# Second edge stage of a graph network: source rows gathered with an add onto spread destination rows in SBUF

## The chip, the cores and the metric

One core of one Trainium2 chip runs the whole program. The time is that of the device, in microseconds, for one execution from inputs in HBM to the output in HBM; the kernel before takes 10617.58 us (median of 3 runs, 10607.35 to 10631.53). Engines are named as in the profile: PE is TensorE, DVE VectorE, ACT ScalarE, POOL GpSimd, SP SyncE, which only issues transfers here.

## The reference, cut to what matters

Two message-passing layers on 12,500 nodes of 160 numbers (64 scalars, 32 vectors of 3) and 200,000 edges sorted by destination. The change lies in the second layer's edge stage, an equivariant attention:

```python
ms = src_s[edge_src] + dst_s[edge_dst]          # per edge: source row + destination row
mv = src_v[edge_src] + dst_v[edge_dst]
w = h @ rw3 + roff                              # weights of the edge, h from an MLP of 64 edge scalars
o0a = w1 * ms
o0b = w4 * (jnp.einsum('eud,ed->eu', mv, Y1) / SQ3)
o1a = (w2 * ms)[:, :, None] * Y1[:, None, :]
o1b = w3[:, :, None] * mv
o1c = w5[:, :, None] * (jnp.cross(mv, Y1[:, None, :]) / SQ2)
ls, lv = _eq_lin(ds, dv, lin_ws, lin_bs, lin_wv)  # ds, dv: the o's side by side
a = jnp.einsum('ehk,hk->eh', _smooth_leaky(alpha), alpha_dot)   # then softmax over the edges of a node
ns = jax.ops.segment_sum(vs * a[..., None], edge_dst, num_segments=n)
```

The two sums of the first lines, 160 numbers per edge, are what is made in another way.

## The kernel before, in words

The stages follow one another: first edge stage (up to about 3530 us), node update (to about 5650 us), second edge stage (5653 to about 9900 us), last node update. The second edge stage is `layer1_edges`. Its edges, padded, are 1568 tiles of 128 edges (R = 128, one edge per SBUF partition). Four tiles (GT = 4) are a sub-batch, eight sub-batches (STEPS = 8) a pass, 49 passes the stage: 392 sub-batches. The first and the last pass are written out, the other 47 are one loop whose body holds eight sub-batches; `At(t, r)` is sub-batch r of pass t, `i.plus(2)` the one two later, and `i.n(...)` the count that a semaphore has to reach.

Nothing schedules this code. Each engine has its own `body`, in program order, and semaphores alone set how the engines stand to one another. `gate` waits for something that has long been true. For one sub-batch i the engines do this:

- SP loads, four sub-batches ahead, the windows `e_win` of destination rows (table TD; L1831, L1832), for every other one h (`e_h`, L1844), and indices and the like now and then; it stores the totals of older sub-batches.
- DVE makes selection matrices (`e_pick`, L1951) for sub-batch i+3.
- PE spreads the destination rows of i+2 over their edges: a selection times a window (`spread_out`, L2124) in two halves of two tiles each, 128 x 320 into PSUM.
- ACT copies each half to SBUF (`keep_far`, L2252), into `e_rows[:, p, 1]`, p being the sub-batch's parity.
- POOL issues four indirect gathers (L1933), one per tile, of 128 source rows of 160 floats (table TS) into `e_rows[:, p, 0]`, and then one multiplication (`weighted`, L1917) for sub-batch i-8. Before the gathers it waits for `added` of i-2, the sign that DVE has used this half of `e_rows`.
- DVE's `sums` adds the two halves of `e_rows` to `e_m` (L1961, 128 x 640, sets `added`), then makes products and cross products with the edge's direction (L1966 to L1974). It does so for i+1. Its `results` for i-1 takes PE's output apart (L2014 to L2030), `weigh` (L1986 to L1992) multiplies PE's weights with `e_m` into `e_d` (sets `d_ready`), and `members` makes `e_q` (L2004).
- PE, after the spreads, turns back the outputs of i-1 (`turn_back`, L2173), makes the weights of i+1 from `e_h` (L2110), waits for `d_ready` of i, turns `e_d` in three groups of transposes (`turn`, L2135), with the totals of i-6 (L2149) between, and applies the linear maps (L2156, L2162, L2163).
- ACT copies out of PSUM: `e_dT` three times and `e_oT` twice (`keep`, L2261), the results (L2281, L2285) and the totals (L2272).

PE's two first groups of `turn` wait for `far_kept` of i+2, since the spreads and the transposes share PSUM banks. What PE, ACT and DVE do follows PE's order closely; POOL's gathers of i are used by DVE two sub-batches later at most.

Of the kernel before, what the change touches and what calls it, by code (L numbers as in the profile page):

```python
# [112 lines left out]
def gate(eng, k):  # L113


    eng.wait_ge(k["ready"], 4)
# [1624 lines left out]
def layer1_edges(nc, m, k, ps, W, TS, TD, index, LR, BASE, iota, dstI, rows_dst, heads_dst, H, yx, TOT):  # L1741

    own = ExitStack()
    with own:
# [7 lines left out]
        hh = sb("e1_h", [128, 2, GT * R])  # L1752
        rows = sb("e1_rows", [R, 2, 2, GT, X])
        m_ = sb("e1_m", [R, 2, GT, X])
        prod, cA, cB, cr = (sb("e1_" + n, [R, GT, 3, V]) for n in ("prod", "cA", "cB", "cr"))
# [11 lines left out]
            "at_here", "row_here", "dh_here", "h_here"))  # L1767
        rows_here = [sem(f"e1_rows_here{p}") for p in range(2)]
        local_here, base_here = ([sem(f"e1_{n}{p}") for p in range(2)] for n in ("local_here", "base_here"))
# [3 lines left out]
        stored = [sem(f"e1_stored{s}") for s in range(STEPS)]  # L1773
        ones_set, added, crossed, mixed, w_ready, d_ready, turned, kept, mapped, outs, by_y, freed = (sem("e1_" + n) for n in (
            "ones_set", "added", "crossed", "mixed", "w_ready", "d_ready", "turned", "kept", "mapped", "outs", "by_y", "freed"))
        silued, logit, xT, apart, masked, forward, scanned, mT, shifted = (sem("e1_" + n) for n in (
# [24 lines left out]
        with nc.Block() as block:  # L1801
            @block.sync
            def _(sp):
# [53 lines left out]
                def body(t):  # L1857
                    final = isinstance(t, int) and t == PASSES - 1
                    for r in range(STEPS):
                        i, ahead = At(t, r), At(t, r).plus(4)  # L1860
                        if ahead.within():
                            gate(sp, k)
                            sp.wait_ge(spread, ahead.n(2, 2, 4))
                            load_windows(ahead)
                        if r % 4 == 0 and not final:
                            load_base(r // 4, t + 1)
                        if r % 4 == 1 and not final:
                            gate(sp, k)
                            sp.wait_ge(picked, i.n(1, 3))
                            load_local(r // 4, t + 1)  # L1870
                        if not (final and r >= 6):
                            gate(sp, k)
                            sp.wait_ge(w_ready, i.n(1, 1))
                            load_h(r % 2, t * 4 + (r // 2 + 1))
                        if r % 4 == 3 and not final:
                            gate(sp, k)
                            sp.wait_ge(added, i.n(1, 1))
                            load_at(r // 4, t + 1)
                        if r % 4 == 2 and not i.before(4) and not (final and r == 6):
                            gate(sp, k)  # L1880
                            sp.wait_ge(scanned, i.groups(0))
                            load_dh(1 - r // 4, t + r // 4)
                        if r % 4 == 1 and not i.before(9):
                            gate(sp, k)
                            sp.wait_ge(q_ready, i.n(1, 1, 6))
                            load_row(r // 4, t)
                        if not i.before(6):
                            gate(sp, k)
                            store(i, 6)
# [19 lines left out]
            def _(pool):  # L1909
# [10 lines left out]
                def body(t):  # L1920
                    for r in range(STEPS):
                        i, p, gp = At(t, r), r % 2, r // 4
                        if r % 4 == 0:
                            gate(pool, k)
                            pool.wait_ge(at_here[gp], i.uses(16, 16))
                        if not i.before(2):
                            gate(pool, k)
                            pool.wait_ge(added, i.n(1, 1, 2))
                        pool.sem_inc(begun, 1)
                        gate(pool, k)  # L1930
                        for c in range(GT):
                            col = 4 * (r % 4) + c
                            pool.indirect_dma_start(rows[:, p, 0, c, :], None, TS, bass.IndirectOffsetOnAxis(  # L1933
                                ap=at[:, gp, col:col + 1], axis=0)).then_inc(rows_here[p], 16)
                        if not i.before(8):
                            weighted(i, 8)
# [5 lines left out]
            def _(dve):  # L1942
# [11 lines left out]
                def sums(i):  # L1954

                    p = i.r % 2
                    gate(dve, k)
                    dve.wait_ge(rows_here[p], i.uses(256, 64 * (i.r // 2) + 64))
                    gate(dve, k)
                    dve.wait_ge(far_kept, i.n(2, 2))  # L1960
                    dve.tensor_tensor(m_[:, p], rows[:, p, 0], rows[:, p, 1], ALU.add).then_inc(added, 1)  # L1961
                    gate(dve, k)
                    dve.wait_ge(added, i.n(1, 1))
                    vec = m_[:, p, :, S:X].rearrange("n c (i u) -> n c i u", i=3)
                    y = [bc(yx[:, j:j + 3, bass.ds(i.n(4), GT)].rearrange("n i c -> n c i"), V, 3) for j in range(3)]
# [10 lines left out]
                def weigh(i):  # L1976

                    p = i.r % 2
                    gate(dve, k)
                    dve.wait_ge(w_ready, i.n(1, 1))  # L1980
                    if not i.before(2):
                        gate(dve, k)
                        dve.wait_ge(turned, i.n(5, 3, 2))
                    vec = m_[:, p, :, S:X].rearrange("n c (i u) -> n c i u", i=3)
                    to = d[:, p].rearrange("r c j x -> r c (j x)")[:, :, S + 128:384].rearrange("r c (i a u) -> r c i a u", i=3, a=2)
                    dve.tensor_tensor(d[:, p, :, 0:2, 0:S], w4[:, :, 0:128].rearrange("r c (a u) -> r c a u", a=2),  # L1986
                                      bc(m_[:, p, :, 0:S], 2, 2), ALU.mult)
                    dve.tensor_tensor(to[:, :, :, 0], bc(w4[:, :, 128:160], 3, 2), vec, ALU.mult)
# [72 lines left out]
                def body(t):  # L2061
                    for r in range(STEPS):
# [4 lines left out]
                        if r % 4 == 1 and not i.before(5):  # L2067
                            scans(i)
                        if i.plus(3).within():
                            selections(i.plus(3))  # L2070
                        if not i.before(1):
# [14 lines left out]
                dve.wait_ge(ones_set, 2)  # L2086
                for r in range(3):
                    selections(At(0, r))
# [10 lines left out]
            def _(pe):  # L2099
# [27 lines left out]
                def turn(i, j):  # L2127
                    p = i.r % 2
                    gate(pe, k)
                    if j < 2 and i.plus(2).within():  # L2130
                        pe.wait_ge(far_kept, i.plus(2).n(2, j + 1))
                    else:
                        pe.wait_ge(kept, i.n(5, j - 1))
# [55 lines left out]
                def body(t):  # L2189
                    for r in range(STEPS):  # L2190
                        i, after = At(t, r), At(t, r + 1) if r + 1 < STEPS else At(t + 1, 0)
                        if i.plus(2).within():
                            spread_out(i.plus(2), 0, far2(i, 0), (far_kept, 3) if i.before(1) else (kept, i.n(5, -1)))
                        if not i.before(1):
                            turn_back(i.plus(-1), 0)
                        if i.plus(2).within():
                            spread_out(i.plus(2), 1, far2(i, 1), (far_kept, 4) if i.before(1) else (kept, i.n(5)))
                        if not i.before(1):
# [19 lines left out]
                pe.wait_ge(ones_set, 2)  # L2218
                for r in range(2):
                    for half in range(2):  # L2220
                        spread_out(At(0, r), half, far2(At(0, 0), half), (far_kept, half + 1) if r else None)
                weights(At(0, 0))
# [10 lines left out]
            def _(act):  # L2233
# [12 lines left out]
                def keep_far(i, half, of):  # L2246
                    gate(act, k)
                    act.wait_ge(spread, i.n(2, half + 1))
                    if half == 0 and not i.before(2):
                        gate(act, k)  # L2250
                        act.wait_ge(added, i.n(1, 1, 2))
                    act.activation(rows[:, i.r % 2, 1, 2 * half:2 * half + 2, :], of, ACT.Copy).then_inc(far_kept, 1)  # L2252

# [33 lines left out]
                def body(t):  # L2287
                    for r in range(STEPS):
                        i = At(t, r)
                        if i.plus(2).within():  # L2290
                            keep_far(i.plus(2), 0, far2(i, 0))
                            keep_far(i.plus(2), 1, far2(i, 1))
                        if not i.before(1):
# [13 lines left out]
                act.preload_act_table_set("exp_and_others")  # L2307
                for r in range(2):
                    for half in range(2):
                        keep_far(At(0, r), half, far2(At(0, 0), half))  # L2310
# [828 lines left out]
```

## Time and profile before

| | |
|---|---|
| median of 3 runs | 10617.58 us |
| profiled execution, first to last instruction | 10684.3 us |
| PE busy | 8950.9 us, 84% |
| DVE busy | 8008.3 us, 75% |
| POOL busy | 6686.3 us, 63% |
| ACT busy | 4828.6 us, 45% |
| mean granted clock of TensorE | 0.925 |

The profiled execution has no time of its own beside the span; the span is 66.7 us above the median of the timed runs. The busy columns are sums over stages with different limits, so they don't say what bounds the second edge stage; the windows view cuts it out. In the rows, "idle before, releaser" is idle time of an engine just before an instruction and what ended it; such a releaser is inferred from semaphore events, and a transfer that has long been over can be named by mistake. The columns of the timeline are start, duration, engine, line, operation, and in brackets the idle time ahead.

### The profile page before, as it was taken

The page shows a single profiled execution, that of the slowest core. Times are in us where ns is not written, and L with a number is a line of the kernel's source. Part 1 is how long each engine was busy: PE and PEld are TensorE (multiplying, and loading weights), DVE is VectorE, ACT ScalarE, POOL GpSimd, SP SyncE. Part 2 cuts the span into 40 slices and gives each one's busy share as a digit, 9 for nine tenths or more (in the row PEclk, how much of TensorE's full clock was granted, in tenths as well). Part 3 has the DMA queues.
Part 4 walks back from the last instruction along what each step waited for, and adds up shares of the span by engine and source line. Part 5 has one row for each costly group of instructions (what it writes and reads, how often), then busy time and mean ns, then how long its engine had stood idle before and what let it go on. Part 6 is the DMA issues. An engine that isn't in the chain of part 4 may idle for free. (4 is left out here: it accounts for less than half of the span.)

```text
span 10684.3 us, 192482 instructions
## 1 busy us (share of the span) xinstructions
PE 8950.9 (84%) x34728; PEld 5257.6 (49%) x34728; DVE 8008.3 (75%) x15400; ACT 4828.6 (45%) x9073; POOL 6686.3 (63%) x4771
## 2 busy tenths in 40 slices
PE   0888888888888799999986888888888888888588
PEld 0444444444444222223225666666666666666233
DVE  3277777777777688888877888888888888888455
ACT  0276666666666211111113444444444444444255
POOL 4488888888888788888873444444444444444231
PEclk5599999999999899999988999999999999999699
DMA  5588888888888999999973444444444444444222
GB/s 202 172 168 171 168 163 169 165 166 169 167 163 162 208 228 224 223 233 230 227 165 105 121 121 121 120 124 124 121 121 122 121 126 121 120 121 123 56 68 52
DMA packets 1081323, 1616.13 MB, mean 151 GB/s; under 512 B 218498, under 2 KB 831885, under 8 KB 1025357
## 3 DMA queue, kind: packets, MB, share of 16 engines
q1 hardware_dynamic: 755862, 1273.87, 43.7%
q0 software_dynamic: 325056, 338.58, 20.2%
q14 instruction: 361, 2.96, 0.1%
q8 instruction: 44, 0.72, 0.0%
HBM read 1533.80 MB, written 444.07 MB: 185 GB/s over the span
## 5 line engine op out<-in xcount | busy, mean ns | idle before, releaser
L442 POOL DMA_INDIRECT sums<-e_total,e_place x1568 | 2493.7, 1590 | 584.8 <-DMA sums<-e_total,e_place 313.9
L1933 POOL DMA_INDIRECT e_rows<-TS,e_at x1568 | 1542.7, 984 | 1738.0 <-DVE e_m L1961 1174.4
L579 PE MATMUL ps<-e_win,e_pick 128*128 128x448 f32 x3136 | 1341.6, 573 | 159.6 <-DVE e_u L476 105.9
L579 PEld LDWEIGHTS ps<-e_win,e_pick 128*128 128x128 f32 x3136 | 620.4, 203 | 917.7 <-issue 832.9
L2261 ACT ACTIVATE e_dT<-ps 128x512 f32<-128x512 f32 x1176 | 671.1, 597 | 841.2 <-PE ps L2135 353.3
L2135 PE MATMUL ps<-ident,e_d 128*128 128x128 f32 x4704 | 663.1, 278 | 300.6 <-ACT e_dT L2261 289.6
L1917 POOL TENSOR_TENSOR e_val<-e_val 128x640 f32<-128x640 f32 x392 | 511.5, 1306 | 523.7 <-ACT e_val L2238 518.0
L1094 POOL TENSOR_TENSOR n_zv<-n_zv,n_ast 128x1536 f32<-128x1536 f32 x200 | 762.9, 3814 | 120.0 <-DMA n_zv<-in_x_groups 107.7
L1299 PE MATMUL ps<-n_z,w_uss 128*64 128x512 f32 x1600 | 748.6, 612 | 20.8 <-DVE n_z L1142 20.1
L2261 ACT ACTIVATE e_oT<-ps 128x512 f32<-128x512 f32 x784 | 469.1, 598 | 627.1 <-PE ps L2163 454.9
L2149 PE MATMUL ps<-e_val,e_q 128*128 128x168 f32 x3136 | 630.7, 327 | 127.6 <-ACT e_tot L2272 108.0
L2135 PEld LDWEIGHTS ps<-ident,e_d 128*128 128x128 f32 x4704 | 547.7, 142 | 382.1 <-ACT e_dT L2261 338.7
L742 DVE SCALAR_TENSOR_TENSOR r_y<-ps,w_rb,r_rstd 128x512 f32<-128x512 f32 x394 | 295.5, 750 | 576.7 <-issue 528.6
L2110 PE MATMUL ps<-w_r,e_h 128*128 128x224 f32 x3136 | 670.3, 357 | 53.5 <-issue 52.0
L2149 PEld LDWEIGHTS ps<-e_val,e_q 128*128 128x128 f32 x3136 | 517.0, 202 | 370.7 <-ACT e_tot L2272 225.5
L1098 POOL TENSOR_TENSOR n_zv<-n_zv 128x512 f32<-128x512 f32 x400 | 668.2, 1670 | 36.9 <-POOL n_zv L1094 0.4
L711 PE MATMUL ps<-r_sq,w_avg 128*128 128x512 f32 x788 | 453.4, 659 | 277.9 <-issue 277.9
L592 PEld LDWEIGHTS ps<-e_u,e_q 128*128 128x128 f32 x3136 | 540.7, 191 | 188.0 <-issue 188.0
L2124 PE MATMUL ps<-e_win,e_pick 128*128 128x160 f32 x3136 | 565.6, 304 | 72.7 <-issue 62.6
L2124 PEld LDWEIGHTS ps<-e_win,e_pick 128*128 128x128 f32 x3136 | 482.4, 194 | 246.8 <-issue 245.5
L620 ACT ACTIVATE e_far<-ps,attr 128x160 f32<-128x160 f32 x1176 | 442.8, 390 | 353.2 <-PE ps L579 214.8
L2110 PEld LDWEIGHTS ps<-w_r,e_h 128*128 128x128 f32 x3136 | 566.5, 191 | 72.3 <-issue 70.8
(438 smaller groups left out, 19874.2 us busy)
## 6 DMA issues: line engine op xcount, KB each, us to landing
e_win<-T SPq DMA_DIRECT2D x1568, 168.0 KB
n_z<-in_x_groups SPq DMA_DIRECT2D x400, 512.0 KB
n_zv<-in_x_groups SPq DMA_DIRECT2D x800, 192.0 KB
TOT<-e_tot SPq DMA_DIRECT2D x392, 352.0 KB
e_row<-in_src_rows SPq DMA_DIRECT2D x98, 1024.0 KB
e_local<-LR SPq DMA_DIRECT2D x196, 512.0 KB
e_row<-in_dst_rows SPq DMA_DIRECT2D x98, 1024.0 KB
e_win<-TD SPq DMA_DIRECT2D x1568, 60.0 KB
```

The costliest lines, as they stand in the source:

```text
L442: pool.indirect_dma_start(sums[c], bass.IndirectOffsetOnAxis(ap=place[:, r % 4, c:c + 1], axis=0), total[:, r % 4, c, 0:MSG0], None, compu ...
L579: pe.matmul(g[:, c, :], pick[:, p, R * c:R * c + R], win[:, s, c, :], start=True, stop=True).then_inc(spread, 1)
L592: last = pe.matmul(out[:, c, :], q[:, p, c, :], u[:, p, c, :], start=True, stop=True)
L1094: pool.tensor_tensor(zv[:, b], zv[:, b], ast[:, g.p], ALU.mult).then_inc(zv_ready, 1)
L1098: pool.tensor_tensor(zv[:, b, 0], zv[:, b, 0], zv[:, b, i], ALU.add).then_inc(zv_ready, 1)
L1299: last = pe.matmul(ps[0:S, U0, :], W["uss"][:, 4 * s + j, :], z[:, s % 4, j, :], start=False, stop=False)
L1933: pool.indirect_dma_start(rows[:, p, 0, c, :], None, TS, bass.IndirectOffsetOnAxis(ap=at[:, gp, col:col + 1], axis=0)).then_inc(rows_here[ ...
L2110: last = pe.matmul(w4[:, c, 0:224], hh[:, p, R * c:R * c + R], W["r3"][:], start=True, stop=True)
L2124: last = pe.matmul(to[:, c % 2], pick[:, p, R * c:R * c + R], win[:, s, c, :], start=True, stop=True)
L2135: last = pe.transpose(ps[:, bank(i, 2 + j), R * c:R * c + R], d[:, p, c, j, :], I[0:R, 0:R])
L2149: last = pe.matmul(tot2[:, c % 2], q[:, j % 2, c, :], val[:, slot // 4, 4 * (slot % 4) + c, :], start=True, stop=True)
L2261: act.activation(to, ps[:, bank(i, 2 + j), :], ACT.Copy).then_inc(kept, 1)
```

## The change

The tile `e_rows` and the semaphore `added` go. `e_m` gets four slots in place of two. ACT copies the spread destination rows straight into the sub-batch's slot of `e_m`. POOL's gathers wait until these copies are made, the first two tiles for the first half, the other two for the second, and write with an add (`compute_op=ALU.add`) onto the slot, so that the DVE instruction L1961 goes. ACT's copy waits for `d_ready` of the sub-batch four back, the last use of the slot. Spreads and their copies move from i+2 to i+3, selections from i+3 to i+4, with one more of each ahead of the first pass. SP's wait for `added` becomes one for `mixed`, which DVE sets after the cross products. Results are otherwise made as before.

```diff
-        rows = sb("e1_rows", [R, 2, 2, GT, X])
-        m_ = sb("e1_m", [R, 2, GT, X])
+        m_ = sb("e1_m", [R, 4, GT, X])
...
-        rows_here = [sem(f"e1_rows_here{p}") for p in range(2)]
+        rows_here = [sem(f"e1_rows_here{s}") for s in range(4)]
...
                         if r % 4 == 3 and not final:
                             gate(sp, k)
-                            sp.wait_ge(added, i.n(1, 1))
+                            sp.wait_ge(mixed, i.n(1, 1))
                             load_at(r // 4, t + 1)
...
-                        if not i.before(2):
-                            gate(pool, k)
-                            pool.wait_ge(added, i.n(1, 1, 2))
-                        pool.sem_inc(begun, 1)
-                        gate(pool, k)
                         for c in range(GT):
+                            if c % 2 == 0:
+                                gate(pool, k)
+                                pool.wait_ge(far_kept, i.n(2, c // 2 + 1))
+                                pool.sem_inc(begun, 1)
+                                gate(pool, k)
                             col = 4 * (r % 4) + c
-                            pool.indirect_dma_start(rows[:, p, 0, c, :], None, TS, bass.IndirectOffsetOnAxis(
-                                ap=at[:, gp, col:col + 1], axis=0)).then_inc(rows_here[p], 16)
+                            pool.indirect_dma_start(m_[:, r % 4, c, :], None, TS, bass.IndirectOffsetOnAxis(
+                                ap=at[:, gp, col:col + 1], axis=0), compute_op=ALU.add).then_inc(rows_here[r % 4], 16)
...
-                    dve.wait_ge(rows_here[p], i.uses(256, 64 * (i.r // 2) + 64))
-                    gate(dve, k)
-                    dve.wait_ge(far_kept, i.n(2, 2))
-                    dve.tensor_tensor(m_[:, p], rows[:, p, 0], rows[:, p, 1], ALU.add).then_inc(added, 1)
-                    gate(dve, k)
-                    dve.wait_ge(added, i.n(1, 1))
+                    dve.wait_ge(rows_here[s], i.uses(128, 64 * (i.r // 4) + 64))
...
-                        if i.plus(3).within():
-                            selections(i.plus(3))
+                        if i.plus(4).within():
+                            selections(i.plus(4))
...
-                    if j < 2 and i.plus(2).within():
-                        pe.wait_ge(far_kept, i.plus(2).n(2, j + 1))
+                    if j < 2 and i.plus(3).within():
+                        pe.wait_ge(far_kept, i.plus(3).n(2, j + 1))
...
-                    if half == 0 and not i.before(2):
+                    if half == 0 and not i.before(4):
                         gate(act, k)
-                        act.wait_ge(added, i.n(1, 1, 2))
-                    act.activation(rows[:, i.r % 2, 1, 2 * half:2 * half + 2, :], of, ACT.Copy).then_inc(far_kept, 1)
+                        act.wait_ge(d_ready, i.n(1, 1, 4))
+                    act.activation(m_[:, i.r % 4, 2 * half:2 * half + 2, :], of, ACT.Copy).then_inc(far_kept, 1)
```

In PE's and ACT's bodies `i.plus(2)` becomes `i.plus(3)` for `spread_out` and `keep_far` in the same way.

On POOL, the start of the loop's body, before. ISA and REGISTER_ALU are waits and register work; `x4` are the four gathers of a sub-batch.

```order
L1925 ISA
L1928 ISA
L1933 DMA e_rows<-TS,e_at 128x160 x4
L1915 ISA
L1917 TENSOR_TENSOR e_val<-e_val 128x32x20
```

The same place after the change:

```order
L1924 ISA
L1928 REGISTER_ALU
L1932 DMA e_m<-TS,e_at 128x160 x2
L1928 REGISTER_ALU
L1932 DMA e_m<-TS,e_at 128x160 x2
L1914 ISA
L1916 TENSOR_TENSOR e_val<-e_val 128x32x20
```

The four gathers keep their place ahead of the multiplication; they are now in two pairs, each behind a wait of its own.

On DVE, one sub-batch from the last instruction of `weigh` to the first of `results`, before:

```order
L1992 TENSOR_TENSOR e_d<-ps,e_dot 128x4x32
L1961 TENSOR_TENSOR e_m<-e_rows 128x640
L1966 TENSOR_TENSOR e_prod<-e_m,yx 128x384
L1967 TENSOR_TENSOR e_cA<-e_m,yx 128x4x64
L1968 TENSOR_TENSOR e_cA<-e_m,yx 128x4x32
L1969 TENSOR_TENSOR e_cB<-e_m,yx 128x4x32
L1970 TENSOR_TENSOR e_cB<-e_m,yx 128x4x64
L1973 TENSOR_REDUCE e_dot<-e_prod 128x128
L1974 TENSOR_TENSOR e_cr<-e_cA,e_cB 128x384
L1951 TENSOR_SCALAR e_pick<-e_local,nodes_sb 128x512
```

And after:

```order
L1986 TENSOR_TENSOR e_d<-ps,e_dot 128x4x32
L1960 TENSOR_TENSOR e_prod<-e_m,yx 128x384
L1961 TENSOR_TENSOR e_cA<-e_m,yx 128x4x64
L1962 TENSOR_TENSOR e_cA<-e_m,yx 128x4x32
L1963 TENSOR_TENSOR e_cB<-e_m,yx 128x4x32
L1964 TENSOR_TENSOR e_cB<-e_m,yx 128x4x64
L1967 TENSOR_REDUCE e_dot<-e_prod 128x128
L1968 TENSOR_TENSOR e_cr<-e_cA,e_cB 128x384
L1950 TENSOR_SCALAR e_pick<-e_local,nodes_sb 128x512
```

The add is gone and nothing else on DVE changes its place; the selection is that of one sub-batch later.

## Rows read from the trace of the kernel before

**Rows 1.** Windows: length, busy us (instructions) of PE, PEld, DVE, ACT, POOL, clock, DMA share, GB/s.

```profile
5660.00:9890.00 4230.00, 3633.11 (x19695) 2839.48 (x19696) 3570.15 (x8683) 2050.17 (x4481) 2043.68 (x1951) 0.97 0.43 121
```

**Rows 2.** Waits, 5660 to 9890: us in total, times, longest us.

```profile
POOL e_rows L1933 <- DVE e_m L1961: 1174.4, 332, 6.9
...
ACT e_dT L2261 <- PE ps L2135: 352.7, 256, 3.6
...
ACT e_dT L2261 <- DMA r_xT<-in_edge_attr: 320.0, 106, 4.1
PE ps L2135 <- ACT e_dT L2261: 289.6, 203, 2.6
...
ACT e_tot L2272 <- remote: 174.8, 95, 3.4
...
ACT e_silu L2281 <- DMA H<-r_h: 126.6, 68, 3.3
...
PE ps L2124 <- DMA e_win<-TD: 10.1, 2, 5.3
```

**Rows 3.** Timeline of one sub-batch of the second edge stage.

```profile
7575.33 1.10 POOL L1933 DMA_INDIRECT e_rows<-TS,e_at  x1 [4.69 <-DVE e_m L1961]
...
7576.83 1.68 PE L2110 MATMUL ps<-w_r,e_h 128*128 128x224 f32 x8
...
7578.35 1.04 PE L2135 MATMUL ps<-ident,e_d 128*128 128x128 f32 x8
...
7579.22 0.74 PE L2149 MATMUL ps<-e_val,e_q 128*128 128x168 f32 x4
7579.25 0.95 POOL L1933 DMA_INDIRECT e_rows<-TS,e_at  x1 [0.30 <-issue]
...
7579.87 0.42 DVE L2030 TENSOR_REDUCE e_val<-e_silu 128x32 f32<-128x256 f32 x1
...
7581.25 1.08 ACT L2261 ACTIVATE e_dT<-ps 128x512 f32<-128x512 f32 x2 [3.46 <-DMA r_xT<-in_edge_attr]
...
7581.35 0.69 DVE L1986 TENSOR_TENSOR e_d<-ps,e_m 128x512 f32<-128x512 f32 x1 [1.06 <-DMA r_xT<-in_edge_attr]
...
7581.90 0.66 PE L2135 MATMUL ps<-ident,e_d 128*128 128x128 f32 x4 [1.95 <-ACT e_dT L2261]
```

**Rows 4.** Timeline of the first edge stage, beside its indirect scatters.

```profile
2006.45 2.05 PE L711 MATMUL ps<-r_sq,w_avg 128*128 128x512 f32 x2 [2.89 <-issue]
...
2007.49 1.55 POOL L442 DMA_INDIRECT sums<-e_total,e_place  x1 [0.30 <-ACT e_total L633]
...
2008.58 0.69 ACT L727 ACTIVATE r_std<-ps,w_eps 128x512 f32<-128x512 f32 x1 [1.36 <-PE ps L711]
```

**Rows 5.** Groups by line, 5660 to 9890: busy, mean ns, idle before and releasers.

```profile
L1933 POOL DMA_INDIRECT e_rows<-TS,e_at x1563 | 1537.9, 984 | 1682.2 <-DVE e_m L1961 1174.4 <-issue 507.8
L1917 POOL TENSOR_TENSOR e_val<-e_val 128x640 f32<-128x640 f32 x388 | 506.2, 1305 | 502.7 <-ACT e_val L2238 497.0 <-issue 0.6
...
L1961 DVE TENSOR_TENSOR e_m<-e_rows 128x640 f32<-128x640 f32 x392 | 373.3, 952 | 0.0
```

**Rows 6.** Indirect scatters by line: duration ns min/median/max, first and last start.

```profile
L442 POOL DMA_INDIRECT sums<-e_total,e_place x1568: 1547/1552/2079, 503.1 to 3520.5; - x196
...
L1115 POOL DMA_INDIRECT TD<-n_rows,n_rank_of x100: 960/1001/2357, 3695.9 to 5597.8; - x100
```

**Rows 7.** DMA queues, 5660 to 9890, then 503 to 3530: packets, MB, share.

```profile
q0 software_dynamic: 75072, 128.22, 12.2%
...
q0 software_dynamic: 225792, 154.24, 47.9%
```

**Rows 8.** DVE L2027 alone, then an instance of it beside POOL's L1917.

```profile
L2027 DVE TENSOR_TENSOR e_silu<-e_silu,w_ad x392: 408/454/2125, 5691.3 to 9904.8; 128x256 f32<-128x256 f32 x196
...
7526.15 1.26 POOL L1917 TENSOR_TENSOR e_val<-e_val 128x640 f32<-128x640 f32 x1
7526.38 1.33 DVE L2027 TENSOR_TENSOR e_silu<-e_silu,w_ad 128x256 f32<-128x256 f32 x1
```

More of the change, by code:

```diff
@@ L1773, in layer1_edges @@
         stored = [sem(f"e1_stored{s}") for s in range(STEPS)]
-        ones_set, added, crossed, mixed, w_ready, d_ready, turned, kept, mapped, outs, by_y, freed = (sem("e1_" + n) for n in (
-            "ones_set", "added", "crossed", "mixed", "w_ready", "d_ready", "turned", "kept", "mapped", "outs", "by_y", "freed"))
+        ones_set, crossed, mixed, w_ready, d_ready, turned, kept, mapped, outs, by_y, freed = (sem("e1_" + n) for n in (
+            "ones_set", "crossed", "mixed", "w_ready", "d_ready", "turned", "kept", "mapped", "outs", "by_y", "freed"))
         silued, logit, xT, apart, masked, forward, scanned, mT, shifted = (sem("e1_" + n) for n in (
@@ L1921, in body @@
                     for r in range(STEPS):
-                        i, p, gp = At(t, r), r % 2, r // 4
+                        i, gp = At(t, r), r // 4
                         if r % 4 == 0:
@@ L1954, in sums @@
                 def sums(i):
-                    p = i.r % 2
+                    s = i.r % 4
                     gate(dve, k)
-                    dve.wait_ge(rows_here[p], i.uses(256, 64 * (i.r // 2) + 64))
-                    gate(dve, k)
-                    dve.wait_ge(far_kept, i.n(2, 2))
-                    dve.tensor_tensor(m_[:, p], rows[:, p, 0], rows[:, p, 1], ALU.add).then_inc(added, 1)
-                    gate(dve, k)
-                    dve.wait_ge(added, i.n(1, 1))
-                    vec = m_[:, p, :, S:X].rearrange("n c (i u) -> n c i u", i=3)
+                    dve.wait_ge(rows_here[s], i.uses(128, 64 * (i.r // 4) + 64))
+                    vec = m_[:, s, :, S:X].rearrange("n c (i u) -> n c i u", i=3)
                     y = [bc(yx[:, j:j + 3, bass.ds(i.n(4), GT)].rearrange("n i c -> n c i"), V, 3) for j in range(3)]
@@ L1976, in weigh @@
                 def weigh(i):
-                    p = i.r % 2
+                    p, s = i.r % 2, i.r % 4
                     gate(dve, k)
@@ L1983, in weigh @@
                         dve.wait_ge(turned, i.n(5, 3, 2))
-                    vec = m_[:, p, :, S:X].rearrange("n c (i u) -> n c i u", i=3)
+                    vec = m_[:, s, :, S:X].rearrange("n c (i u) -> n c i u", i=3)
                     to = d[:, p].rearrange("r c j x -> r c (j x)")[:, :, S + 128:384].rearrange("r c (i a u) -> r c i a u", i=3, a=2)
                     dve.tensor_tensor(d[:, p, :, 0:2, 0:S], w4[:, :, 0:128].rearrange("r c (a u) -> r c a u", a=2),
-                                      bc(m_[:, p, :, 0:S], 2, 2), ALU.mult)
+                                      bc(m_[:, s, :, 0:S], 2, 2), ALU.mult)
                     dve.tensor_tensor(to[:, :, :, 0], bc(w4[:, :, 128:160], 3, 2), vec, ALU.mult)
@@ L2086, in _ @@
                 dve.wait_ge(ones_set, 2)
-                for r in range(3):
+                for r in range(4):
                     selections(At(0, r))
@@ L2191, in body @@
                         i, after = At(t, r), At(t, r + 1) if r + 1 < STEPS else At(t + 1, 0)
-                        if i.plus(2).within():
-                            spread_out(i.plus(2), 0, far2(i, 0), (far_kept, 3) if i.before(1) else (kept, i.n(5, -1)))
+                        if i.plus(3).within():
+                            spread_out(i.plus(3), 0, far2(i, 0), (far_kept, 5) if i.before(1) else (kept, i.n(5, -1)))
                         if not i.before(1):
                             turn_back(i.plus(-1), 0)
-                        if i.plus(2).within():
-                            spread_out(i.plus(2), 1, far2(i, 1), (far_kept, 4) if i.before(1) else (kept, i.n(5)))
+                        if i.plus(3).within():
+                            spread_out(i.plus(3), 1, far2(i, 1), (far_kept, 6) if i.before(1) else (kept, i.n(5)))
                         if not i.before(1):
@@ L2218, in _ @@
                 pe.wait_ge(ones_set, 2)
-                for r in range(2):
+                for r in range(3):
                     for half in range(2):
-                        spread_out(At(0, r), half, far2(At(0, 0), half), (far_kept, half + 1) if r else None)
+                        spread_out(At(0, r), half, far2(At(0, 0), half), (far_kept, 2 * r + half - 1) if r else None)
                 weights(At(0, 0))
@@ L2289, in body @@
                         i = At(t, r)
-                        if i.plus(2).within():
-                            keep_far(i.plus(2), 0, far2(i, 0))
-                            keep_far(i.plus(2), 1, far2(i, 1))
+                        if i.plus(3).within():
+                            keep_far(i.plus(3), 0, far2(i, 0))
+                            keep_far(i.plus(3), 1, far2(i, 1))
                         if not i.before(1):
@@ L2307, in _ @@
                 act.preload_act_table_set("exp_and_others")
-                for r in range(2):
+                for r in range(3):
                     for half in range(2):
```

## The prediction

> **What bounds the kernel now.** I read the windows view first, to see which engine fills the stage that is changed. The second edge stage runs from 5660 to 9890 us, 4230 us for 392 sub-batches of four tiles, so 10.79 us each [rows 1]. TensorE (PE) is busy 3633 us of it, 9.27 us per sub-batch, at a granted clock of 0.97, the upper level of 2.4 GHz but for 3%. VectorE (DVE) is busy 9.11 us, GpSimd (POOL) 5.21 us, ScalarE (ACT) 5.23 us. So PE is nearest to the bound and stands idle for 1.52 us per sub-batch; what the change is worth is decided by what happens to those 1.52 us, since PE's own 9.27 us stay.
>
> Next I read the waits of that stage, to see what PE's idle time ends with. PE waits for ACT's copies (L2261), 290 us in 203 of the sub-batches [rows 2]. It hardly waits for DVE: no such row is near the top. ACT in turn waits 353 us for PE's transposes (L2135), and 320, 175 and 127 us are put down to transfers of the first edge stage or to nothing named ("r_xT", "remote", "H"). Those transfers ended long before, so these are semaphore events whose sender the trace could not pair. They sum to 622 us, 1.59 us per sub-batch, which is PE's idle time over again.
>
> The timeline of one sub-batch says what they are [rows 3]. PE ends its two groups of transposes (L2135) at 7579.39. ACT should copy them at once, but starts at 7581.25 after 3.46 us of idling, and DVE, which needs PE's products of L2110 (ended 7578.51), starts e_d at 7581.35, though its last reduction was over by about 7580.3. PE, which needs ACT's copies, stands from 7579.96 to 7581.90. Both late starts come 1.05 to 1.15 us after POOL's last gather instruction ended (7579.25 + 0.95 = 7580.20). So: while the four gathers of a sub-batch flow, PE's finished work is told late to its consumers, and it is told about 1 us after the last gather was issued. I call this the hold. Beside the first edge stage's indirect scatters it is not seen: there a PE matmul (L711) ends at 2008.50 while a scatter is under way, and its consumer on ACT starts at 2008.58 [rows 4].
>
> **The change, part by part.**
>
> *The add on DVE goes.* 392 x 952 ns = 373 us of DVE's time [rows 5], 0.95 us per sub-batch. Nothing on PE waits for DVE as it is, so at 10.79 us per sub-batch it is worth 0; it would count only if PE's loss went first (rival 1). DVE's next limit is then 9.11 - 0.95 = 8.16 us busy.
>
> *The gathers become accumulating ones.* The trace has no gather with an add. A plain gather takes POOL 984 ns; the nearest row with an add is the first stage's scatter (L442), 1552 ns as median, 1590 as mean, while a plain scatter (L1115) takes 1001 ns [rows 5, 6]. I take 1.55, with bounds of 0.95 (the add is free on POOL) and 2.5 (the longest plain scatter, 2.36 [rows 6], rounded up). With 0.30 us from one to the next [rows 3, 4] four take 7.40 us instead of 4 x 1.25 = 5.0 us, and with the weighting L1917 (1.26 + 0.30) POOL comes to 8.96 us of 10.79: it still fits.
>
> *Their transfers.* 5660 to 9890: the software queue has 12.2% of 16 engines, 0.122 x 16 x 4230 / 1563 = 5.28 engine-us per gather of 80 KB. The accumulating scatters: 0.479 x 16 x 3027 / 1568 = 14.8 for 96 KB, 12.3 scaled to 80 KB [rows 7]. The DMA share goes from 0.43 to about 0.12 x 12.3/5.28 + 0.31 = 0.59: not a bound, and a gather's share of the 16 engines (0.77 us) is shorter than its issue.
>
> *The order of arrival.* POOL now waits for ACT's copies of the same sub-batch instead of DVE's add of the one two before. POOL waited 1174 us for that add [rows 2], so it was early anyway. Behind the waiting gather stand on POOL the other gathers and L1917, whose product PE wants two sub-batches on. The gathered rows are needed by DVE's sums two sub-batches on, over 10 us later: no loss. ACT's copy waits for d_ready four sub-batches back, long past; the rings hold.
>
> *One sub-batch further ahead.* PE's spread (L2124), ACT's copy and DVE's selection have the same count and place, only a later sub-batch as object; the first pass has one more of each ahead of it, about 3 us once, in which POOL no longer gathers. The windows are asked for by SP four sub-batches ahead and now needed one earlier. They are waited for 10 us in all now, the last of [rows 2]; I take 0 to 0.1 us per sub-batch.
>
> *The hold.* This is the term that decides. The train of four gathers lasts now from 7575.33 to 7580.20, 4.87 us. With 1.55 us each it lasts 4 x 1.55 + 3 x 0.30 = 7.10 us, 2.23 more; its first issue ends 0.60 later, so that the stretch in which PE's news is late grows by 1.6 us. As much as 1.6 us per sub-batch could be lost once more; now the loss is 1.52 us on a stretch of 4.87 + 1.05 - 1.10 = 4.8 us, a third, and a third of 1.6 is 0.5. PE waits for ACT in 203 of 392 sub-batches [rows 2], about half: half of 1.6 is 0.8, to which I add 0.1 for sub-batches newly caught and for the windows. Value taken: 0.9 us, x 392 = 353 us. Bounds: 0.3 (the longer stretch falls mostly on PE's long runs without a consumer) and 2.1 (all of 1.6, and 0.5 of stalls of DVE beside L1917, which now follows the last gather at another place: L2027 took 1.33 us beside it in place of 0.45 [rows 8]).
>
> Here the Trainium skill speaks against my reading. *SBUF — State Buffer*, section *Who interferes with whom*, has it that DMA never contends with a compute engine and that "PE and ACT never wait on anyone". In rows 3 ACT starts 1.86 us after PE's end and within 1.1 us of the last gather's, which no port explains; if the rule covered semaphores too, the lateness would be something else's, the longer train would cost nothing, and the result would be rival 2's. The trace here does not agree with so wide a reading of it.
>
> **Sum.** Beside the profiled execution, 10684.3 us of span and 66.7 us (0.6%) above the median of the runs, it is 10684 + 353 = 11037; against the median it is 10617.6 + 353 = **10,970 us**. With its bounds, 118 to 823 us: 10,740 to 11,440.
>
> **The rivals.**
>
> *Rival 1, faster: the accumulating gathers hold nothing.* The scatters with an add don't [rows 4], plain gathers do, and an accumulating gather is as much of the one as of the other. Then PE's loss of 1.52 us mostly goes. The floors are PE 9.27, POOL 8.96, DVE 8.16 plus its dependences; with 0.6 us left of ordinary waits the period is 9.9: -0.89 x 392 = -350 us, 10,270 us. For it: the hold was seen only beside gathers that write SBUF without an add. Against it: these write SBUF too, and the train is longer.
>
> *Rival 2, no change: the hold keeps its size or isn't the gathers'.* If it follows the bytes (80 KB each, unchanged) rather than the issue time, all terms are hidden: 10,600, within 60.
>
> *Rival 3, slower still: POOL becomes the bound.* 4 x (t + 0.30) + 1.56 passes 10.79 at t = 2.0 us. The plain scatter has a maximum of 2.36 [rows 6]. At t = 2.5 the period is 12.8, +2.0 x 392 = +780 us, 11,400 us. Every us over the threshold counts fourfold.
>
> **Chances.** Forecast 0.50, rival 1 0.27, rival 2 0.18, rival 3 0.05. A difference under 0.2%, 21 us, can't be told from none. The forecast and rival 3 are slower whole; rival 1 is faster whole; rival 2 I split 0.08 faster, 0.06 same, 0.04 slower. That makes faster 0.35, same 0.06, slower 0.59. The likeliest case's own range is 10,740 to 11,440; with rival 1's middle 10,260 to 11,450, which leaves out the faster half of rival 1 and the end of rival 3.
>
> **What would show it.** In the profile after: the gather with a mean near 1.55 us on POOL (under 1.1: the add is free, and the train is as before; over 2.0: rival 3, POOL near 100%); the software queue's share near 28% in this stage; DVE's busy time lower by 373 us; PE's the same 3633 us. The forecast is right if PE idles 2.4 us per sub-batch, the mislabelled waits of ACT grow to near 2.5 us per sub-batch, and ACT's late copies still start about 1 us after the last gather of each train. It is wrong if ACT starts within 0.2 us of PE's end while gathers are under way (rival 1), or if the period stays at 10.8 with the train at 7.1 us (rival 2).

## The result, and the profile after

The changed kernel takes 10058.99 us (median of 4 runs, 10040.0 to 10064.59), against 10616.4 for the kernel before: 0.947 of it, 95% interval 0.9457 to 0.9484. Forecast were 10,970 us and 3.3% more; it is 5.3% less. Rival 1 came closest, and even its 10,270 us lies 210 us too high. Timed once more among the experiments, the changed kernel came to 0.948 of before (0.9458 to 0.9505).

The windows view of the kernel after, columns as in [rows 1]:

```profile
5660.00:9300.00 3640.00, 3433.72 (x19723) 2780.57 (x19723) 3518.78 (x8308) 2092.36 (x4487) 3080.42 (x1956) 1.00 0.64 142
```

The stage is over some 600 us earlier. PE is busy almost throughout, at the upper clock level all the time (1.00, was 0.97), DVE too, and POOL, half idle before, is now full but for the gaps between its instructions. The gathers' tile says how the period fell: from (9867.9 - 5653.3) / 391 = 10.78 us to (9274.5 - 5662.3) / 391 = 9.24 us. Columns as in [rows 6], before and after:

```profile
L1933 POOL DMA_INDIRECT e_rows<-TS,e_at x1568: 942/949/1262, 5653.3 to 9867.9; - x196
...
L1932 POOL DMA_INDIRECT e_m<-TS,e_at x1568: 1540/1566/1982, 5662.3 to 9274.5; - x196
```

The waits of the kernel after, 5660 to 9270, columns as in [rows 2]:

```profile
POOL e_m L1932 <- issue: 461.5, 1531, 2.1
ACT e_dT L2255 <- PE ps L2129: 353.2, 289, 2.4
...
PE ps L2129 <- ACT e_dT L2255: 2.0, 5, 0.4
```

The waits of [rows 2] that named transfers of another stage, "r_xT", "remote" and "H", 622 us in all, are not in the list any more, and PE's 290 us of waiting for ACT have become 2. That is the lateness of PE's news, gone. The timeline of one sub-batch shows PE and ACT beside the accumulating gathers:

```profile
7583.02 1.82 POOL L1932 DMA_INDIRECT e_m<-TS,e_at  x1 [0.62 <-issue]
...
7584.44 1.04 PE L2129 MATMUL ps<-ident,e_d 128*128 128x128 f32 x8
...
7585.08 1.09 ACT L2255 ACTIVATE e_dT<-ps 128x512 f32<-128x512 f32 x2 [1.23 <-PE ps L2129]
7585.15 1.89 POOL L1932 DMA_INDIRECT e_m<-TS,e_at  x1 [0.31 <-issue]
```

ACT begins to copy the first group while PE still turns the second, in the middle of the train of gathers; in [rows 3] it began 1.86 us after PE had ended both. Over the whole trace it is the same: of the 1176 copies of e_dT none starts more than 0.1 us after both PE's group and ACT's own instruction before it have ended. In the kernel before 261 start more than 0.5 us late, the latest 3.1 us.

Last, the groups by line, 6000 to 9000, where DVE's e_q is new among the long ones:

```profile
L1998 DVE TENSOR_TENSOR e_q<-e_row,dstI 128x512 f32<-128x512 int32 x324 | 575.6, 1776 | 0.0
...
L1916 POOL TENSOR_TENSOR e_val<-e_val 128x640 f32<-128x640 f32 x324 | 552.9, 1707 | 60.5 <-ACT e_val L2232 60.5
```

e_q took 0.73 us before (`L2004`), the multiplication 1.30 [rows 5]. They now stand beside each other in about three of four sub-batches (e_q is over 0.9 us in 258 of 335 between 5900 and 9000 us), and it is e_q that waits. One such place:

```profile
7589.44 1.56 POOL L1932 DMA_INDIRECT e_m<-TS,e_at  x1 [0.30 <-issue]
...
7589.87 2.97 DVE L1998 TENSOR_TENSOR e_q<-e_row,dstI 128x512 f32<-128x512 int32 x1
...
7590.43 1.85 POOL L1916 TENSOR_TENSOR e_val<-e_val 128x640 f32<-128x640 f32 x1
```

The multiplication's record begins 0.57 us before that of the last gather ends (7591.00). From there it takes 1.28 us, and in every sub-batch from 5900 to 9000 between 1.25 and 1.29: its mean of 1.71 is the overlap of two records of POOL, not a slower multiplication.

### The profile page after: what moved, and what is told of

It reads as the page before. It is cut to its first block and busy times, and to the rows that moved or that the text cites. A ratio compares the mean times of both kernels' runs of the same rounds, so it can differ in the third digit from the quotient of the medians.

```text
span 10062.5 us, 191932 instructions
## 1 busy us (share of the span) xinstructions
PE 8731.8 (87%) x34728; PEld 5186.5 (52%) x34728; DVE 7958.4 (79%) x15008; ACT 4874.1 (48%) x9073; POOL 7733.9 (77%) x4771
## 5 line engine op out<-in xcount | busy, mean ns | idle before, releaser
L1932 POOL DMA_INDIRECT e_m<-TS,e_at x1568 | 2582.3, 1647 | 529.2 <-issue 462.4
L1916 POOL TENSOR_TENSOR e_val<-e_val 128x640 f32<-128x640 f32 x392 | 667.0, 1702 | 101.1 <-ACT e_val L2232 101.1
L1098 POOL TENSOR_TENSOR n_zv<-n_zv 128x512 f32<-128x512 f32 x400 | 689.4, 1723 | 36.8 <-POOL n_zv L1094 0.4
L1998 DVE TENSOR_TENSOR e_q<-e_row,dstI 128x512 f32<-128x512 int32 x392 | 684.6, 1747 | 13.3 <-PE ps L2143 13.3
L2129 PE MATMUL ps<-ident,e_d 128*128 128x128 f32 x4704 | 641.9, 273 | 3.5 <-ACT e_dT L2255 2.0
L2143 PEld LDWEIGHTS ps<-e_val,e_q 128*128 128x128 f32 x3136 | 496.8, 193 | 198.0 <-issue 153.4
L2143 PE MATMUL ps<-e_val,e_q 128*128 128x168 f32 x3136 | 586.1, 310 | 8.0 <-ACT e_tot L2266 7.5
L592 PE MATMUL ps<-e_u,e_q 128*128 128x194 f32 x3136 | 583.7, 329 | 0.0
```

What stands on the lines that cost most here:

```text
L592: last = pe.matmul(out[:, c, :], q[:, p, c, :], u[:, p, c, :], start=True, stop=True)
L1098: pool.tensor_tensor(zv[:, b, 0], zv[:, b, 0], zv[:, b, i], ALU.add).then_inc(zv_ready, 1)
L1916: pool.tensor_tensor(u[:, :, 1:SEG], u[:, :, 1:SEG], bc(u[:, :, 0], SEG - 1, 2), ALU.mult).then_inc(u_ready, 1)
L1932: pool.indirect_dma_start(m_[:, r % 4, c, :], None, TS, bass.IndirectOffsetOnAxis(ap=at[:, gp, col:col + 1], axis=0), compute_op=ALU.add). ...
L1998: dve.tensor_tensor(q[:, j % 2], row[:, gp, R * cols.start:R * cols.stop].rearrange("r (c e) -> r c e", c=GT), bc(dstI[:, 0, bass.ds(i.n(4 ...
L2143: last = pe.matmul(tot2[:, c % 2], q[:, j % 2, c, :], val[:, slot // 4, 4 * (slot % 4) + c, :], start=True, stop=True)
```

## The experiments

All ratios are to the kernel before on the same chip, with 95% intervals; a point is 1% of the time before. The period is read from the count of a line in a window of 3000 us. The diffs show the lines that change, shortened. "Late copies" are counted over each whole trace as above: copies of e_dT, of 1176, that start more than 0.5 us after both PE's group and ACT's instruction before have ended.

**Is it the kind of gather?** `e1_after_plain` leaves the add out of the gathers.

```diff
-   ap=at[:, gp, col:col + 1], axis=0), compute_op=ALU.add).then_inc(rows_here[r % 4], 16)
+   ap=at[:, gp, col:col + 1], axis=0)).then_inc(rows_here[r % 4], 16)
```

> The changed kernel with gathers that don't add: they overwrite the spread rows, so the destination rows are missing from the sums. All else (ring of four, spreads three ahead, POOL's waits on ACT's copies, no add on DVE) stays. Theory K (the kind of transfer: a plain gather holds PE's news, an accumulating one doesn't): the hold is back, PE idles again by about 1.5 us per sub-batch; period about 10.3 to 10.8, total 10,480 to 10,650 us. Rival O (the new order, waits and ring removed the loss): the stage stays at 9.2 us per sub-batch or falls, since a gather takes POOL 0.98 us in place of 1.65: 9,900 to 10,060 us.

Measured: 1.031 (1.0293 to 1.0328). Neither range of the expectation holds it: theory K had 10,480 to 10,650 us, and it is 11,010, slower than the kernel before. The new order with plain gathers loses 3.1%, and the late news is back, with 402 late copies. Timeline of it:

```profile
7581.73 1.04 PE L2129 MATMUL ps<-ident,e_d 128*128 128x128 f32 x8
7582.36 0.60 ACT L2255 ACTIVATE e_dT<-ps 128x512 f32<-128x512 f32 x1 [1.28 <-issue]
...
7584.13 0.95 POOL L1932 DMA_INDIRECT e_m<-TS,e_at  x1 [0.30 <-issue]
7584.65 0.60 ACT L2255 ACTIVATE e_dT<-ps 128x512 f32<-128x512 f32 x1 [1.70 <-PE ps L2129]
```

PE's second group ended at 7582.77, and ACT copies it at 7584.65, with the last gather of the train issued at 7584.13. POOL now starts behind ACT's copy of the spreads, so that the train should stand at the same critical place each time: ACT waits for PE's transposes 425 times up to 9200 us, 256 in [rows 2]. That this place is the reason for the extra loss was not tried.

`e2_before_add` puts the add into the gathers of the kernel before; their tile is cleared once, ahead of the stage, and nothing else changes.

```diff
-   ap=at[:, gp, col:col + 1], axis=0)).then_inc(rows_here[p], 16)
+   ap=at[:, gp, col:col + 1], axis=0), compute_op=ALU.add).then_inc(rows_here[p], 16)
...
+   for p in range(2):
+       pool.memset(rows[:, p, 0], 0.0).then_inc(cleaned, 1)
+   pool.wait_ge(cleaned, 2)
```

> The kernel before with an add in its gathers (onto e_rows' own half, cleared once, so the rows pile up and the values are not the reference's); DVE's add, its waits and the ring of two stay. Theory K: the hold goes, PE no longer idles for it; what is left is DVE with its add, 8.98 + 0.95 = 9.9 us per sub-batch, total 10,150 to 10,350 us. Rival O: the loss stays and the longer trains add to it, 10,620 us or more.

Measured: 1.005 (1.0031 to 1.0065): no gain from the gathers alone. The number is rival O's, its reason isn't: the loss did not stay, there are no late copies. Neither theory named what took its place; groups by line, 6000 to 9000:

```profile
L2008 DVE TENSOR_TENSOR e_q<-e_row,dstI 128x512 f32<-128x512 int32 x274 | 657.1, 2398 | 0.0
```

e_q has 2.40 us in place of 0.73. DVE is busy 2886 of 3000 us; it sets the period of 10.95 us, with PE at 9.4.

**Is it the spacing?** `e3_before_paced`: plain gathers, a fill on POOL after each.

```diff
+   if not (i.before(1) and c == 0):
+       gate(pool, k)
+       pool.wait_ge(filled, i.n(4, c))
+       pool.sem_inc(begun, 1)
+       gate(pool, k)
...
+   pool.memset(filler[:], 0.0).then_inc(filled, 1)
```

> The kernel before with plain gathers, but after each of them POOL fills a 128x256 tile nobody reads, so that a gather starts only every 1.9 to 2.2 us, as the accumulating ones do. Theory K: plain gathers hold at any pace; over a longer stretch, no gain: 10,620 to 11,100 us (this is also the step of my forecast, a longer train costs more: 10,900). Rival P (pace: the hold comes from gathers that follow each other too closely): most of the gain appears, 10,100 to 10,350 us.

Measured: 0.984 (0.9817 to 0.9857), 1.6% faster, against theory K and against the step of my forecast, and less than rival P. There are no late copies, but DVE is busy 2879 of 3000 us: POOL's multiplication now falls beside DVE's add (1.26 us in place of 0.95) and e_prod (1.23 in place of 0.56). The clean comparison needs DVE relieved; it is `e9_after_plain_paced`, the kernel of e1 with the same edit and a fill of 64 columns.

> The changed kernel with plain gathers (the destination rows are overwritten and missing, as in e1_after_plain, which took 1.031 of before) and after each a fill of 128x64 on POOL, so that they start about every 2.0 us in place of 1.3. Theory P (the spacing of the gathers, not their kind, decides whether PE's news is late): the hold goes, 0.945 to 0.965 of before, close to the changed kernel's 0.947. Rival K (the kind): 1.00 to 1.05.

Measured: 0.944 (0.9408 to 0.9467). POOL and ACT in its timeline:

```profile
7579.35 0.96 POOL L1939 DMA_INDIRECT e_m<-TS,e_at  x1 [3.35 <-issue]
7580.31 0.17 POOL L1941 MEMSET e_filler<- 128x64 f32 x1
...
7581.31 0.95 POOL L1939 DMA_INDIRECT e_m<-TS,e_at  x1 [0.82 <-POOL e_filler L1941]
...
7584.22 1.04 PE L2137 MATMUL ps<-ident,e_d 128*128 128x128 f32 x8
...
7584.86 1.09 ACT L2263 ACTIVATE e_dT<-ps 128x512 f32<-128x512 f32 x2 [1.19 <-PE ps L2137]
```

Same gathers, same order of everything else as e1; only 2.0 to 2.1 us from start to start in place of 1.3: 1.031 becomes 0.944, a little better even than theory P's range, and 402 late copies become none (the latest is 0.2 us late). Theory P holds, theory K falls: no accumulating gather is needed for the gain; it is slower to issue, and so spaced. How close is too close, `e14_plain_pairs` asks, with the fill after the second and fourth gather only (`if c % 2 == 1:`).

> As e9_after_plain_paced (plain gathers, destination rows missing, a start every 2.0 us, 0.944 of before), but POOL's fill of 128x64 only after the second and the fourth gather: they follow in pairs, 1.3 us within a pair and 2.0 us between. Theory P with all gathers counting alike: half the cost of close gathers comes back, 0.98 to 1.00. Rival: two close gathers hold nothing, only a train of four does: 0.935 to 0.95, POOL having more time. Other rival: one close pair is as bad as four: 1.02 or more.

Measured: 0.957 (0.9551 to 0.9583), between e9 and e1 and in none of the three ranges expected: of the 8.7 points from e9 to e1 pairs bring back 1.3. There are 11 late copies. A train of four close ones costs far more than two trains of two.

The late copies also settle a rival of the spacing, that the fills only move the train to a place where it does no harm. In e14 259 of PE's groups came due after the third gather, the first of the second pair, and none was copied late; in the kernel before 167 came due after the third gather of the train, and 129 were.

**What is DVE's add worth?** `e5_before_noadd` cuts it to two columns in the kernel before, `e6_paced_noadd` in e3; the sums are then constants, set once.

```diff
-   dve.tensor_tensor(m_[:, p], rows[:, p, 0], rows[:, p, 1], ALU.add).then_inc(added, 1)
+   dve.tensor_tensor(m_[:, p, :, 0:2], rows[:, p, 0, :, 0:2], rows[:, p, 1, :, 0:2], ALU.add).then_inc(added, 1)
...
+   dve.memset(m_[:], 1.0)
```

> The kernel before with DVE's add cut to two columns of each tile (the products then read constants: the sums are left out). Gathers stay plain and quick, one every 1.3 us. What the first runs left as theory PD: two limits lie over each other, the hold of PE's news (gone as soon as gathers start about 2 us apart) and DVE (with its add 10 us per sub-batch once it also stalls beside POOL). Then taking the add alone gives nothing: 0.98 to 1.01 of before. Rival A: the add was the main cost, most of the gain of 5.3% appears: 0.95 to 0.97.

> The same cut of the add, with the plain gathers spaced by POOL's fills as in the third run (which alone gave 0.984). No accumulating transfer, no ring of four, no spread further ahead is in it. Theory PD: both limits are gone, period 9.2 to 9.5 us, 0.945 to 0.96 of before, as the whole change. Rival K2: something of the change itself (the kind of transfer, the ring, the lead) is needed: 0.97 to 0.99.

Measured: 0.989 (0.9867 to 0.991) and 0.962 (0.9602 to 0.9642). The add alone is worth 1.1%, more than the nothing that I had, less than rival A; the late news stays in e5 (279 late copies). With spacing it is worth 2.2 points (0.984 to 0.962), with no late copies. e6 misses 0.945 to 0.96 by a little: with fills of 256 columns its gathers start 2.1 to 2.25 us apart, and the next train 3.3 us after the fourth, which makes up the period of 9.8 us; and POOL's multiplication falls beside DVE's e_cA, 1.56 us in place of 0.42. `e7_after_extra_add` gives the changed kernel such an add back, unread.

```diff
+   dve.tensor_tensor(extra[:], m_[:, s], m_[:, s], ALU.add).then_inc(added, 1)
+   gate(dve, k)
+   dve.wait_ge(added, i.n(1, 1))
```

> The changed kernel with an extra DVE addition of 128x640 ahead of the products, where before had its add, with the same wait behind it; nobody reads its result. Theory PD: DVE goes from 9.07 to over 10 us per sub-batch and sets the period: 10.1 to 10.9 us, 0.98 to 1.01 of before. Rival B: POOL, full at 4 x 1.95 + 1.4 us, is the bound of the changed kernel and DVE's stalls beside it are slack: below 0.965.

Measured: 0.962 (0.9592 to 0.9644), just inside rival B's range and far from theory PD's. 0.54 us of the add's 0.86 show in the period; e_q's mean falls from 1.78 to 1.33 us at the same time, so that a part of the add fills what was a stall.

**The stall beside POOL's multiplication.** `e11_before_add_w_small` and `e10_after_w_small` cut the multiplication in e2 and in the changed kernel.

```diff
-   pool.tensor_tensor(u[:, :, 1:SEG], u[:, :, 1:SEG], bc(u[:, :, 0], SEG - 1, 2), ALU.mult
+   pool.tensor_tensor(u[:, :, 1:3], u[:, :, 1:3], bc(u[:, :, 0], 2, 2), ALU.mult
```

> The kernel before with accumulating gathers (e2_before_add, 1.005 of before at 10.96 us per sub-batch, DVE busy 10.7 with 1.5 us of stall in e_q beside POOL's multiplication), with that multiplication cut in the same way. Theory S (the gain was hidden by that stall, since POOL's wait for DVE's add puts the multiplication beside e_q): DVE falls to 9.2 to 9.5, 0.955 to 0.975 of before. Rival (the ring of two or the order of waits costs it): above 0.985.

> The changed kernel with POOL's multiplication cut from 20 to 2 columns of each head (most of the weighting is left out). It gives back about 1 us per sub-batch on POOL and DVE's stall of 1.0 us in e_q beside it. Theory Q (POOL is the bound of the changed kernel, with PE's 8.75 us just under it): period 8.8 to 8.95, 0.93 to 0.94 of before. Rival (PE's chain is the bound): 0.944 to 0.95.

Measured: 0.948 (0.9446 to 0.9508) in place of 1.005, better than theory S's range, and 0.940 (0.9368 to 0.9425) in place of 0.947, the edge of theory Q's. Group by line of e11:

```profile
L2008 DVE TENSOR_TENSOR e_q<-e_row,dstI 128x512 f32<-128x512 int32 x324 | 242.5, 748 | 0.0
```

With e_q back at 0.75 us the kernel before, given accumulating gathers, runs as fast as the changed one with its add on DVE still there. So the stall hid the gain in e2. In the changed kernel it and POOL's fullness cost 0.7%. (The cut also frees 0.7 to 0.8 us of POOL; the two aren't told apart.)

**Versions meant to be faster.** Three put the multiplication elsewhere in POOL's order: `e4_after_mid` ahead of the third gather, `e13_after_w_c3` ahead of the fourth (both in three of four sub-batches), `e12_three_one` behind the second, which is plain and added by DVE. `e8_hybrid` takes two gathers plain, the second and the fourth, and DVE adds them. The edit of e4:

```diff
+   if c == 2 and r % 4 != 0 and not i.before(8):
+       weighted(i, 8)
...
-   if not i.before(8):
+   if r % 4 == 0 and not i.before(8):
        weighted(i, 8)
```

> The changed kernel with POOL's multiplication moved between the second and the third gather in three of four sub-batches, away from DVE's e_q (L1998), which takes 1.77 us in place of 0.74 since both read SBUF. Theory D (after the change POOL and DVE bound each other: POOL is full, DVE 97%): e_q falls to below 1.1 us, the multiplication to 1.3, period 9.21 to about 9.0, total 9,950 to 10,010 us. Rival: PE with 8.8 us busy and its chain sets the period, total within 20 us of 10,059.

> The changed kernel with POOL's multiplication ahead of the fourth gather in three of four sub-batches, so that it should fall beside DVE's weigh, whose instructions read one operand from PSUM, and not beside e_q. e10_after_w_small (0.940) is what could be had at most. Theory S (what the multiplication meets on DVE decides): e_q below 1.1 us, 0.940 to 0.945 of before, under e15_after_again. Rival R (POOL's start drifts against DVE, so that no fixed place in POOL's order avoids DVE's two-operand instructions): 0.948 to 0.96, as with the other two places tried.

> A version meant to be faster: of the changed kernel's four gathers the second is plain, into a tile of its own that DVE adds (128x160), and POOL's multiplication follows it in three of four sub-batches. Every gather still starts 1.9 us or more after the one before. By theory P and Q: POOL 8.6, DVE 8.4 plus at most 0.5 of stall, PE 8.75: period 8.9 to 9.1, 0.935 to 0.943 of before. Rival (the multiplication meets DVE's two-operand instructions at the new place as it did in e4_after_mid): 0.95 or more.

> The changed kernel with tiles 0 and 2 gathered with the add, tiles 1 and 3 plain into a tile of their own and added by DVE (128x320, about 0.5 us). POOL saves 2 x 0.6 = 1.2 us per sub-batch of 9.26, plain and accumulating gathers alternate at 1.3 and 1.9 us. Theory PD: if a mean spacing of 1.6 us still holds nothing, the period goes to 8.9 us, PE's: 0.935 to 0.945 of before. Rival: every plain gather followed after 1.3 us holds PE's news again: 0.97 to 1.02.

Measured: 0.956 (0.9537 to 0.9576), 0.955 (0.953 to 0.9562), 0.963 (0.9603 to 0.9662), 0.951 (0.9482 to 0.9534). None beats the changed kernel, and none is in the range that its theory hoped for; e12 and e13 are in their rivals'. e8 has the late news again: 159 late copies, up to 1.8 us, all of them after its third gather, which accumulates and starts some 1.3 us after a plain one. So a gather with an add, when it follows closely, spares nothing. The changed kernel ran beside e13 as `e15_after_again`:

> The changed kernel itself, to have it beside the next two on one chip: 0.944 to 0.950 of before by every theory.

Measured: 0.948 (0.9458 to 0.9505). Groups by line of e13, 6000 to 9000:

```profile
L2000 DVE TENSOR_TENSOR e_q<-e_row,dstI 128x512 f32<-128x512 int32 x316 | 403.1, 1276 | 0.0
L2023 DVE TENSOR_TENSOR e_silu<-e_silu,w_ad 128x256 f32<-128x256 f32 x315 | 277.3, 880 | 0.0
```

e_q is relieved by half a microsecond, and L2023, another instruction with both operands in SBUF, gets as much more (0.88, 0.42 in the changed kernel). The stall moved, it didn't go: DVE has such instructions in several places, and POOL drifts against DVE. POOL also waits for ACT's copies in e13 (207 us of 3000), which it hardly did (4 us).

## Why the prediction was wrong

- **What bounds the kernel** was read rightly: PE's 1.52 us of idling per sub-batch were late news of PE, tied to the gathers, and they are what went. PE idles 0.5 us now (3000 - 2837 us over 324 sub-batches), where the forecast had 2.4.
- **The step that failed is "The hold".** It said that the stretch of late news lasts as long as the train, so that a longer train costs more (+0.9 us). PE's idle time fell by 1.0 us where this term had it grow by 0.9. The runs show that a longer train of the same four gathers is spaced wider, and that spacing removes the loss (1.031 to 0.944, 402 late copies to none). The rows couldn't tell "as long as gathers flow" from "as long as they follow closely": all trains of the kernel before had one spacing, 1.3 us. What I did have was the first stage, where the scatters with an add start 1.86 us apart (the one of [rows 4] at 2007.49 stands between the two below) and hold nothing in the place shown there; I took it as the kind's doing (rival 1) and not the spacing's. For the changed kernel rival 1 gives the right direction, for another cause.

```profile
2005.63 1.55 POOL L442 DMA_INDIRECT sums<-e_total,e_place  x1 [0.30 <-DMA sums<-e_total,e_place]
...
2009.35 1.55 POOL L442 DMA_INDIRECT sums<-e_total,e_place  x1 [0.30 <-issue]
```

- **The size of rival 1** was short by 210 us. It kept PE at 9.27 us and added 0.6 us of waits. PE's busy time fell to 8.76 (2837 / 324). Most of it is the clock, which rose from 0.97 to 1.00: in the kernel before the lower level (0.5, 1.2 GHz) was granted for 287 us of the stage, and L2156 takes 1005 ns in those stretches and 625 outside them. Summed over PE's lines, that costs 0.4 us per sub-batch (an estimate from such differences). The floor that was taken as fixed was not.
- **The add on DVE "worth 0"** held for PE's waits, not quite for the time: 1.1% alone, 2.2 once the hold is gone. The text had it that it counts when PE's loss goes first.
- **POOL's price** was right in kind: 1.55 us forecast, 1.65 mean, 1.57 median; software queue 29.1% of the engines where 28% was said. With 4 x 1.95 = 7.8 us, a multiplication of 1.28 us and 0.2 us of waiting for ACT ahead of it, POOL is full in a period of 9.26; 8.96 was the forecast.
- **DVE beside L1917** was a side remark with 0.5 us as its price. It is a term of its own: 1.0 us per sub-batch of e_q's time in the changed kernel, 1.65 in e2, enough there to hide the whole gain. The rule of the Trainium skill, *SBUF — State Buffer*, *Who interferes with whom*, that a DVE instruction with two SBUF inputs contends with a GpSimd instruction that reads SBUF, agrees with e11 (e_q back at 0.75 us) and e13 (L2023 at 0.88). Its sentence that DMA never contends with a compute engine doesn't cover what e1 against e9 shows (1.031 against 0.944).
- **The arrival and the lead** were harmless as said: DVE waited for gathers 12 us, PE for windows 4 us.

Open: by what path close gathers make PE's finished work known late, and whether only PE's. The runs fix when it happens, not how; nor do they say why e8's close pairs (159 late copies) do more than e14's (11). Why plain gathers in the new order lose more than in the old with its add cut (1.031 against 0.989) is argued from where the train stands, and was not tried alone.

## What to carry to other kernels

Where waits name impossible senders and end just after a train of gathers, try the spacing of that train first: 2.0 us from start to start in place of 1.3 was worth 8.7 points here (e1 to e9), with the same bytes. In the kernel before, spacing alone was worth 1.6 points (e3): DVE was the next limit. An edit can be worth nothing (e2) because a second limit takes its gain at once, so test edits in pairs, and read what each engine meets on the others, not only its busy time.

## What the runs showed of the hardware

- Beside four plain indirect gathers of 80 KB issued 1.3 us apart, ACT starts on PE's finished work up to 3.1 us late in the kernel before (261 of 1176 copies over 0.5 us late); issued 2.0 to 2.1 us apart (e9), at most 0.2 us late. Gathers with an add behave the same: none late at 1.9 us (changed kernel, e2), 159 where one follows a plain gather after 1.3 us (e8).
- An indirect gather with an add onto SBUF takes POOL 1.55 us, and 1.82 and 1.89 in the timeline above, beside DVE's instructions on e_m; that these are the cause was not tried. A plain one takes 0.95.
- A tensor_tensor of 128x512 on DVE beside one of 128x640 on POOL, all operands in SBUF, is stretched from 0.73 us to means of 1.78 (changed kernel) and 2.40 (e2), at most 3.0; POOL's takes its 1.28 us as without it (1.26 in e9).
